# Graph network kernel: half of the hop matrix's chunk loads moved from SyncE's DMA queue to ScalarE's

## What is computed

```
# three hops over the same weighted graph, and their mean
emb = acc = h                                  # h: 6250 x 64
for _ in range(3):
    msgs = edge_weight[:, None] * emb[src]
    emb = segment_sum(msgs, dst)               # 6250 x 64
    acc = acc + emb
x = x + acc / 4
```

## Time and profile before

| | |
|---|---|
| median of three runs | 8540.25 us |
| profiled execution, its own time | 8541.52 us |
| its span | 8539.8 us |
| busy: PE, POOL, DVE, ACT | 5791.4, 4978.0, 4682.3, 1529.0 us |
| hop stage, from the first load's issue to the last turn's end | 4834.0 to 6320.3 us |
| mean granted TensorE clock | 0.669 of full speed |

### The profile page before, as it was taken

The page is one execution under the profiler, slowest core; times in us unless marked ns, Lnnn a source line. Parts: engine busy times, 40 slices in busy tenths (PEclk is TensorE's granted clock), DMA queues, the critical chain, the costliest instruction groups (busy, mean ns, idle before and its releaser), DMA issues.

```text
span 8539.8 us, 133569 instructions
## 1 busy us (share of the span) xinstructions
PE 5791.4 (68%) x42197; PEld 4230.6 (50%) x42197; DVE 4682.3 (55%) x10280; ACT 1529.0 (18%) x4329; POOL 4978.0 (58%) x5265
## 2 busy tenths in 40 slices
PE   2177777777768555555554477777777777787777
PEld 1166666666653555545554222222235555555555
DVE  3388898898981676666674200000015555555555
ACT  1111111111112111111110000000013333333333
POOL 0277777777751777777777510111107777777776
PEclk9565565555565666666665599999976666666666
DMA  5555555555543444444443499999963333333332
GB/s 100 94 92 90 89 93 90 91 91 90 92 88 126 68 70 68 71 68 71 67 72 49 134 426 427 397 426 397 426 254 83 83 81 82 82 82 82 81 82 68
DMA packets 803401, 1178.96 MB, mean 138 GB/s; under 512 B 623063, under 2 KB 656279, under 8 KB 775466
## 3 DMA queue, kind: packets, MB, share of 16 engines
q1 hardware_dynamic: 630458, 923.60, 35.7%
q0 software_dynamic: 172528, 250.20, 15.9%
HBM read 921.76 MB, written 258.23 MB: 138 GB/s over the span
## 4 chain that ended last, share of the span: by engine, by line
POOL 49%; issue 20%; DMA 16%; PE 11%; DVE 2%; SPq 1%; ACT 0%; POOLq 0%; DVEq 0%; ACTq 0%
POOL arena L493 48%; DMA arena<-B_d 12%; PE ps L913 5%; DMA arena<-tab,idx 2%; PE ps L816 2%; PE ps L858 1%; DMA attr_s<-arena 1%; PE ps L809 1%; POOL recb L502 1%; PE ps L845 1%; DMA emb_d<-pair 0%; PE ps L940 0%; SPq L371 0%; PE ps L975 0%; PE ps L798 0%
## 5 line engine op out<-in xcount | busy, mean ns | idle before, releaser
L493 POOL DMA_INDIRECT arena<-tab,idx x4992 | 4730.1, 948 | 1888.8 <-issue 1650.3
L858 PE MATMUL ps<-arena 128*128 128x64 f32 x6656 | 1347.7, 387 | 1100.0 <-DMA arena<-tab,idx 1038.3
L858 PEld LDWEIGHTS ps<-arena 128*128 128x128 f32 x6656 | 1283.5, 296 | 1185.7 <-issue 926.7
L845 PE MATMUL ps<-arena 128*64 128x98 f32 x15872 | 1370.1, 350 | 436.6 <-DVE arena L1217 430.3
L845 PEld LDWEIGHTS ps<-arena 128*64 128x64 f32 x15872 | 1155.8, 207 | 598.3 <-DVE arena L1217 549.2
L913 PE MATMUL ps<-arena,ev 128*64 128x512 f32 (+1 forms) x4836 | 1110.0, 605 | 370.5 <-DMA arena<-B_d 293.7
L1215 DVE TENSOR_TENSOR arena<-arena,ps 128x784 f32<-128x784 f32 x992 | 957.3, 965 | 0.0
L913 PEld LDWEIGHTS ps<-arena,ev 128*64 128x64 f32 x4836 | 382.6, 143 | 1097.7 <-issue 750.9
L531 POOL DMA_INDIRECT ev<-emb_d,dvI x186 | 175.3, 943 | 1260.2 <-PE ps L913 1045.2
L1176 DVE TENSOR_TENSOR arena<-relT,ps 128x1024 f32<-128x1024 f32 x624 | 759.4, 1217 | 198.4 <-issue 195.5
L1282 DVE COPY pair<-ps 128x512 f32<-128x512 f32 x9 | 5.7, 685 | 1440.4 <-PE ps L913 1440.4
(11 more groups left out here) (211 smaller groups left out, 3891.7 us busy)
## 6 DMA issues: line engine op xcount, KB each, us to landing
arena<-B_d SPq DMA_DIRECT2D x186, 3136.0 KB, 17.1
B_d<-stg SPq DMA_DIRECT2D x248, 784.0 KB
arena<-tab,idx POOLq DMA_INDIRECT x4992
arena<-rel_d SPq DMA_DIRECT2D x208, 256.0 KB
tab<-arena SPq DMA_DIRECT2D x26, 1024.0 KB, 3.8
attr_s<-arena SPq DMA_DIRECT2D x13, 512.0 KB, 9.8
stg<-attr_s SPq DMA_DIRECT2D x208, 32.0 KB
rec_d<-arena SPq DMA_DIRECT2D x6, 832.0 KB, 27.4
```

The lines of the kernel that those rows point to most:

```text
L493: pool.indirect_dma_start(gat[:, r, k * width:(k + 1) * width], None, table, bass.IndirectOffsetOnAxis(ap=idx[:, r, k:k + 1], axis=0)).the ...
L845: ins = pe.matmul(ps[3 + j % 2][a * KP:(a + 1) * KP, i2 * KC:(i2 + 1) * KC], Lw[:, j % 2, t, :], Rc[:, j % 2, t, :], start=True, stop=True)
L858: ins = pe.matmul(ps[6 + r % 2][:, k * D:(k + 1) * D], S[:, r % 2, k, :], gat[:, r, k * D:(k + 1) * D], start=True, stop=True)
```

## The change

Of the 186 chunk loads SyncE keeps those with even u. Those with odd u are issued by ScalarE, with the same wait and the same semaphores, from its own DMA queue. ScalarE issues u = 1 to 63 ahead of its copies after hop 0, u = 65 to 125 ahead of those after hop 1, u = 127 to 185 ahead of those after hop 2. Since the first of them stands behind ScalarE's `std(0, NB)`, it can be issued only after the square root of the layer norm before the hops. ScalarE also waits once for the chunks of B_d to have been written, as SyncE does.

```diff
@@ block.sync
-                    wait(sp, s_["hop_mm"], u - BUFS + 1)
-                    sp.dma_start(Bb[:, u % BUFS, :], B_d[c * P * COLS:(c + 1) * P * COLS].rearrange("(p x) -> p x", p=P)).then_inc(b_in[u % BUFS], 16)
+                    if u % 2 == 0:
+                        wait(sp, s_["hop_mm"], u - BUFS + 1)
+                        sp.dma_start(Bb[:, u % BUFS, :], B_d[c * P * COLS:(c + 1) * P * COLS].rearrange("(p x) -> p x", p=P)).then_inc(b_in[u % BUFS], 16)
@@ block.scalar
             std(0, NB)
+            assert NCH % 2 == 0
+            for h in range(2):
+                act.wait_ge(b_out[h], NCH * 2 * 16)
             for m in range(NH):
+
+                for u in range(m * NCH + (1 if m == 0 else 3), min((m + 1) * NCH + 3, NH * NCH), 2):
+                    c = u % NCH
+                    wait(act, s_["hop_mm"], u - BUFS + 1)
+                    act.dma_start(Bb[:, u % BUFS, :], B_d[c * P * COLS:(c + 1) * P * COLS].rearrange("(p x) -> p x", p=P)).then_inc(b_in[u % BUFS], 16)
                 act.wait_ge(s_["hop_mm"], (m + 1) * NCH)
```

## The result

The changed kernel takes 8585.71 us (median of five runs, 8583.44 to 8589.19) against 8540.25 us: slower by 45 us, ratio 1.0054, 95% interval 1.0039 to 1.0068. The forecast was 8542.5 us with a range to 8558.

A forecast was written before the change was run, and what follows sets the result against it. The hops were taken to be bound by the 16 DMA engines' joint rate. Terms 0.5 + 0 + 0 + 1.8 = +2.3 us on the profiled 8541.5 gave 8543.8, or 8542.5 us against the median; range 8530 to 8558.

The forecast's parts named there:

- What bounds the kernel: In the hops: the 16 DMA engines' joint rate is the bound, not the queue feeding them; 17.1 us shows only line length.
- Issuing: 93 load issues of 0.33 us move from SyncE to ScalarE, which has idle time: no cost on either.
- The middle of a hop: Mid-hop: two chunks share the engines equally, one still lands every 7.61 us, same bytes and rate: 0 us.
- The start: Before the first hop: the embedding's write meets the end of ScalarE's first load: +0.5 us, bounds 0 and +4.0.
- Between hops: Two gaps: the embedding's write is issued 3.7 us later but lands at the same time: 0 us, bounds 0 and +3.7 each.
- The cover of 12.4 us: Between hops: time the write stood behind chunks 63 and 64 anyway, of which a 3.7 us later issue uses part.
- The end: Last two turns: chunks 184 and 185 share, 184 landing 3.7 us ahead of 185: +1.8 us, bounds -1.7 and +3.5.
- the slower one: All turns: mixing two queues costs rate, 0.155 us a turn, 29 us, 8571 us; decides from 7.70 us a turn; 12%.
- first two signs of being wrong: In the hops: a mid-hop rate off 426 by more than 5 GB/s; turns in pairs with long gaps.
- Taking turns: In the engines: each takes a packet from each queue in turn, so chunks in flight finish half a chunk apart.
- The ceiling of 435.2 GB/s: Faster rival, gather turns: a second queue fills gaps, 25 us, 8517 us; by this ceiling an estimated 26 us; 8%.

The follow-up runs named there:

- act_all: Kernel before, with all 186 chunk loads moved to ScalarE's queue and the embedding's write left on SyncE's: 8540.48 us, ratio 1.000.
- halves_two: Kernel before, each chunk loaded as two column halves, one by SyncE, one by ScalarE: 8554.04 us, ratio 1.0015; both halves by SyncE: 8553.81 us.
- experiment 3: Kernel before, with only the embedding's write between hops issued by ScalarE, all chunk loads on SyncE: 8539.65 us, ratio 0.9999.
- mid_two: Changed kernel, banks 5 and 6 multiplied from other data, place given back after bank 4: 8546.66 us against 8524.89 for the kernel before, same chip.
- early_two: Changed kernel, banks 3 to 6 multiplied from other data, place given back after bank 2: 8549.25 us against 8541.64 for the kernel before, same chip.
- early_one: Kernel before, one queue, banks 3 to 6 multiplied from other data, place given back after bank 2: 8542.01 us, ratio 0.9999.

## Why the prediction was wrong, point by point

- **What bounds the kernel**: right. The hops are bound by the rate of the engines; the queue's 17.1 us said nothing of the speed. act_all confirms that no issuer was the limit.
- **Issuing, 0 us**: right; 93 issues of 0.33 us on ScalarE delay nothing.
- **The middle of a hop, 0 us**: this step failed, by 48 us. It said that a load comes "up to 1 us late", and that the other queue "still has half a chunk, 3.7 us, to transfer". The rate was to stay the same because that cover is longer than the lateness. Both rest on chunks that land evenly, 7.61 us apart, and they don't. They land in bunches, and of two that land together the second is multiplied only after the first, at 5.6 us a turn, or some 8.2 to 8.6 at a mixed clock. So its place comes back late: from a chunk's last packet to the issue into its place it was 8.65 us at the median in the middle of the hops, against 7.46 before. 101 loads were issued after their queue had run empty, 2.8 us late at the median and not up to 1. A term stood in the prediction at nothing: the time from issue to the first packet, some 1 us with free engines and 3.4 beside a busy queue. Together the queue stood empty for 5.05 us at the median of these loads, against an assumed cover of 3.7; what was left beside it ranged widely (a lowest tenth of 2.5 us), and where it was short the engines ran out of packets.
- With one queue a load is issued hardly sooner, 7.46 us after that last packet, but the load before it in the same line is then only beginning; only 3 of 185 loads found the queue empty. At a chunk's last packet in mid-hop the loads already issued had one or two whole chunks left to transfer in the kernel before (1.6 in the mean), and 1.0 at the median in the changed one, with 0.5 in the lowest tenth; with the early release it was 1.5, which is what even sharing would give.
- I also treated the 16 engines as one. In the changed kernel 8 to 15 packets are under way for 101 us, so some engines have work while others have none. That one engine is done with both chunks while others are not fits this, but the records don't name the engine, so it is argued. The missing packets make up 20 of the 47.5 us; the rest is in longer packets, at the start of loads above all, for which the prediction had no term either.
- **The start, +0.5 us**: +1.6 us, within the bounds, but not by sharing. No chunk packet starts while the write's packets run. Its first packet started 1.7 us after the issue instead of 0.8, and from first to last they took 5.75 us instead of 5.03.
- **Between hops, 0 us**: +0.8 and -5.1 us. The second write's first packet started 5.6 us after its issue, where it had been 8.2; in the first gap it was 9.8, where it had been 8.0. So less of the chunks' bytes stood ahead of the second write; a small gain that was not foreseen. The cover of 12.4 us that I gave the write was read too long, too: in the kernel before its packets begin 8.0 us after the issue.
- **The end, +1.8 us**: -1.7. From the start of turn 184 to the first copy it took 13.3 us instead of 15.0, since the last turn took 5.58 us and not 7.28. The two turns started 7.65 us apart, as with one queue, not half a chunk apart; load 185 was issued 5.4 us after load 184, so they shared little:

```profile
6357.44 5.58 PE L922 MATMUL ps<-arena,ev 128*64 128x512 f32 x26 [0.33 <-DMA arena<-B_d]
6365.09 5.58 PE L922 MATMUL ps<-arena,ev 128*64 128x512 f32 x26 [2.07 <-DMA arena<-B_d]
```

- **The rivals**: the slower one had the right sign, and the beat went past its deciding 7.70 us a turn (426 / 413 x 7.61 gives 7.85), but it had the wrong mechanism. A price per switch of queue would have shown in halves_two. The right rival, a late load on a queue with too little behind it, stood in the working as a cover and was not turned round into a rival. Both of the prediction's first two signs of being wrong came: a rate off 426 by more than 5 GB/s, and turns in pairs with long gaps.
- **Taking turns**: that each DMA engine takes packets from the queues in turn (the Trainium skill, "DMA: Bandwidth & Descriptors", Queues, rings and completion order) agrees with the packets in the write's gap in experiment 3, 97 of the chunks' beside 128 of the write's. The ceiling of 435.2 GB/s (the Trainium skill, "DMA: Bandwidth & Descriptors", Where 436 GB/s comes from) was not approached by a second queue: 426 in mid-hop at best.

## What to carry to other kernels

In this case a load stream that already kept the DMA engines full gained nothing from a second issuing queue, and with three places it lost. With three places and two queues, one of the queues mostly has a single load, and a place that comes back late leaves that queue empty. Before splitting such a stream, compare how long a queue will stand empty (here 5.05 us in the late loads, of which up to 3.4 are from issue to first packet) with what the other queue has left (half a chunk, 3.7 us, at even sharing, and less in the lowest tenth here). Giving the place back sooner cured it here; a fourth place might as well, but was not tried. If one transfer must be spread over two queues, split each transfer rather than alternate them; that kept the order and cost nothing here beyond its smaller packets.

## What was not expected of the hardware

- A busy share of 0.99 with 3% less moved, and of 1.01 in the halved loads at 422 GB/s: the share counts packets' time, and the packets had grown longer (960 ns in the mean instead of 944; two halves 956).
- A load's first packet starts 0.96 us after its issue when the engines are free, and some 3.4 us after it beside another queue at work.
- Packet size matters even at this size: pieces of 12,544 bytes instead of 25,088, in twice as many loads, cost 1% of the rate (422 against 426 GB/s) and 13 us, with one queue or two.
- A transfer on a queue of its own overtook little: 1664 KB took 15.3 us beside chunk loads, against 16.3 behind them in one line. It began 3.5 us after its issue, and its packets, smaller than the chunks', took turns with theirs.
- TensorE's granted clock in mid-hop fell from 0.95 to between 0.87 and 0.91 in the three full-length kernels with uneven turns (after, mid_two, early_two), and was 0.94 in halves_two and 0.95 in early_one. The same amount of work, unevenly spaced, got a lower mean clock; where places came back early, the whole kernel lost some 8 us by the medians.
